# A cross-attention block: the residual add goes from VectorE to GpSimd, the layer norms' statistics follow a step later, and the expert choice takes fewer instructions

## The reference

```python
x = x + tanh(g_xattn[0]) * xattn(layernorm(x), ctx, ctx, bias, ...)     # 16 heads of 16, bias [128, 16, 128, 128]
#   scores = q_h @ k_h.T / 4 + bias;  p = softmax(scores);  out = p @ v_h   (q, k, v with low-rank terms)
x = x + tanh(g_ffn[0]) * ffn(layernorm(x))
#   expert = argmax(softmax(x @ Wg + bg));  out = gelu(x @ W1[e] + b1[e]) @ W2[e] + b2[e]
```

## Time and profile before

| | us |
|---|---|
| median of 3 runs (lowest, highest) | 1483.44 (1481.97, 1483.55) |
| the profiled execution's own time | 1482.58 |
| its span, from the first to the last instruction | 1480.4 |
| TensorE busy | 1367.4 (92%) |
| VectorE busy | 1079.3 (73%) |
| GpSimd busy | 962.8 (65%) |
| ScalarE busy | 904.5 (61%) |
| first scores start at | 33.92 |
| last scores start at | 1117.61 |

### The profile page before, as it was taken

The page is one execution under the profiler, slowest core; times in us unless marked ns, Lnnn a source line. Parts: engine busy times, 40 slices in busy tenths (PEclk is TensorE's granted clock), DMA queues, the critical chain, the costliest instruction groups (busy, mean ns, idle before and its releaser), DMA issues.

```text
span 1480.4 us, 43554 instructions
## 1 busy us (share of the span) xinstructions
PE 1367.4 (92%) x13462; PEld 1144.0 (77%) x13462; DVE 1079.3 (73%) x2591; ACT 904.5 (61%) x1915; POOL 962.8 (65%) x1062
## 2 busy tenths in 40 slices
PE   6999999999999999999999999999995589999997
PEld 4778787888788877878787778887774468888886
DVE  4888888888888888888888888888886423333333
ACT  2677777777777777777777777777764223333332
POOL 3657777777777777777777777777776234444444
PEclk7999999999999999999999999999998799999999
DMA  7455566556556556655655655655650578888884
GB/s 198 120 167 165 163 176 176 159 170 181 157 168 176 166 161 175 174 160 173 176 158 168 183 158 166 176 167 161 179 148 32 177 242 268 258 261 261 259 254 120
DMA packets 350771, 264.79 MB, mean 179 GB/s; under 512 B 18007, under 2 KB 313335, under 8 KB 350714
## 3 DMA queue, kind: packets, MB, share of 16 engines
q1 hardware_dynamic: 337130, 228.61, 54.4%
q0 software_dynamic: 13056, 34.63, 6.3%
q10 hardware_dynamic: 528, 0.84, 0.2%
HBM read 226.88 MB, written 39.22 MB: 180 GB/s over the span
## 4 chain that ended last, share of the span: by engine, by line
PE 48%; DVE 23%; issue 17%; ACT 3%; POOL 3%; SPq 3%; DVEq 1%; DMA 1%; POOLq 0%; ACTq 0%
DVE sc L829 9%; PE bank L486 8%; PE bank L637 7%; PE bank L623 7%; PE bank L479 6%; PE bank L464 5%; PE bank L566 4%; PE bank L531 2%; PE bank L516 2%; DVE st L850 2%; PE bank L612 2%; DVE x L928 2%; POOL x2n L402 2%; DVE negmax L835 2%; DVE CNT L879 2%
## 5 line engine op out<-in xcount | busy, mean ns | idle before, releaser
L381 POOL TENSOR_TENSOR sc<-sc,negmax 128x1024 f32<-128x1024 f32 x256 | 485.3, 1896 | 178.8 <-DVE negmax L835 175.8
L829 DVE TENSOR_TENSOR sc<-bank,sc 128x512 f32<-128x512 f32 x512 | 328.6, 684 | 99.9 <-PE bank L464 95.2
L835 DVE TENSOR_REDUCE negmax<-sc 128x8 f32<-128x1024 f32 x256 | 312.4, 1220 | 17.0
L685 ACT ACTIVATE PT<-bank 128x512 f32<-128x512 f32 x512 | 278.2, 598 | 0.2
L479 PE MATMUL bank<-cst,sc 128*128 128x128 f32 x2048 | 272.5, 276 | 0.0
L433 POOL DMA_INDIRECT out<-og,ids x144 | 141.7, 984 | 181.2 <-issue 158.9
L479 PEld LDWEIGHTS bank<-cst,sc 128*128 128x128 f32 x2048 | 225.5, 141 | 25.5 <-issue 25.5
L994 DVE SCALAR_TENSOR_TENSOR og<-bank,tg,sc 128x512 f32<-128x512 f32 x72 | 54.1, 751 | 196.6 <-PE bank L637 192.8
L416 POOL DMA_INDIRECT rows_dram<-x2n,slot_i x128 | 138.6, 1083 | 59.0 <-issue 55.1
L669 ACT ACTIVATE KT<-bank,bk_half,cst 128x256 f32<-128x256 f32 x256 | 123.7, 563 | 52.6 <-PE bank L486 52.6
L464 PE MATMUL bank<-KT,QT 32*128 32x256 f32 x2048 | 146.6, 400 | 1.0 <-ACT x2T L721 0.4
(11 more groups left out here) (134 smaller groups left out, 2193.3 us busy)
## 6 DMA issues: line engine op xcount, KB each, us to landing
sc<-in_bias SPq DMA_DIRECT2D x256, 512.0 KB, 4.9
xg<-rows_dram SPq DMA_DIRECT2D x72, 272.0 KB, 3.4
w_sb<-in_w SPq DMA_DIRECT2D x72, 257.0 KB, 3.9
sc<-in_w SPq DMA_DIRECT2D x72, 256.0 KB
x_sb<-in_x SPq DMA_DIRECT2D x128, 128.0 KB, 2.0
ctx_sb<-in_ctx_in SPq DMA_DIRECT2D x128, 128.0 KB, 4.9
rows_dram<-vacant SPq DMA_DIRECT2D x9, 272.0 KB, 3.1
out<-og,ids POOLq DMA_INDIRECT x144, 3.9
```

The lines of the kernel that those rows point to most:

```text
L381: nc.gpsimd.tensor_tensor(s, s, m, ALU.add).then_inc(sub_ok, 1)
L685: nc.scalar.activation(PT[:, t.slot(2), 512 * q:512 * q + 512], b_t[q % 2][:], ACT.Exp).then_inc(pt_ready, 1)
L829: nc.vector.tensor_tensor(s, b_s[q][:], s, ALU.add).then_inc(s_used, 1)
L835: nc.vector.tensor_reduce(negmax[:, t.slot(2), 8 * h:8 * h + 8], sc[:, t.slot(4), 1024 * h:1024 * h + 1024].rearrange("p (h k) -> p h k", ...
```

## The change

1. VectorE's product with the reciprocals (L922) is written to `x2` in SBUF instead of to PSUM. The residual add (L928) leaves VectorE; GpSimd does it, in place, behind its two subtractions, and signals `x2_ok` from there. TensorE's next use of that PSUM bank waits for the product (`y_ok`) alone.
2. VectorE takes the second norm's statistics not of `done` at the end of a step but of `old` in the step after, behind the bias adds of quarters 0 and 1 and ahead of the first row maximum.
3. GpSimd computes scale and shift first in its step, for lags -4 and 3 in place of -5 and 2, and subtracts the maxima after that.
4. ScalarE applies both norms behind the exponentials of quarters 0 and 1, not ahead of the OT copy.
5. The expert choice runs on the lag 4 and lag 5 steps themselves, its instructions set between VectorE's others: a maximum, a comparison, two running sums (`tensor_tensor_scan`) and a product take the place of ten instructions. The one-hot and the counts lie in two halves of `tally` that alternate.
6. In the set-up, GpSimd does three steps instead of two ahead of its memsets.

```diff
+        lmax, best = sb("lmax", [P, 4]), sb("best", [P, 4, EXPERTS])
+        run = sb("run", [P, 4 * EXPERTS])
+        tally = sb("tally", [P, 2, 44])
+        SEEN = [tally[:, 1 - g, 4:44] for g in range(2)]
+        SUMS = [tally[:, g, 0:40] for g in range(2)]
+        OH = [z.rearrange("p (e j) -> p j e", j=5)[:, 1:5, :] for z in SEEN]
+        CNT = [z.rearrange("p (e j) -> p j e", j=5) for z in SUMS]
...
         def norms_at(i, k):
 
-            which = [n for n, lag in enumerate((-5, 2)) if seq(i, k, lag)]
+            which = [n for n, lag in enumerate((-4, 3)) if seq(i, k, lag)]
             return (which[0], which[-1] + 1) if which else None
 
...
             def step(i, k):
-                cur = seq(i, k, 0)
-                if cur:
-                    subtract_max(cur, 0)
-                    subtract_max(cur, 1)
-                norms = norms_at(i, k)
+                cur, done, norms = seq(i, k, 0), seq(i, k, 2), norms_at(i, k)
                 if norms:
-                    here, row = At(i, k, U), (k - 2) % 8
-                    ahead, done = seq(i, k, -5), seq(i, k, 2)
-                    if done and done.reached(8):
-                        pool.wait_ge(x2_out[row], done.per(8, 16))
-                    if ahead:
-                        pool.wait_ge(mv_ok[0], ahead.n(1, 1))
-                    if done:
-                        pool.wait_ge(mv_ok[1], done.n(1, 1))
+                    here, row = At(i, k, U), (k - 3) % 8
+                    nxt, old = seq(i, k, -4), seq(i, k, 3)
+                    if old and old.reached(8):
+                        pool.wait_ge(x2_out[row], old.per(8, 16))
+                    if nxt:
+                        pool.wait_ge(mv_ok[0], nxt.n(1, 1))
+                    if old:
+                        pool.wait_ge(mv_ok[1], old.n(1, 1))
                     pool.nop(nofuse=True)
...
-                    pool.wait_ge(ve_ok, here.n(1, 6))
+                    pool.wait_ge(ve_ok, here.n(1, 5))
...
-                    pool.wait_ge(rs_ok, here.n(1, 6))
+                    pool.wait_ge(rs_ok, here.n(1, 5))
...
+                if cur:
+                    subtract_max(cur, 0)
+                    subtract_max(cur, 1)
+                if done:
+                    pool.wait_ge(y_ok, done.n(1, 1))
+                    nc.gpsimd.tensor_tensor(x2[:, done.slot(2), :], x2[:, done.slot(2), :], x_sb[:, done.slot(8), :],
+                                            ALU.add).then_inc(x2_ok, 1)
...
-            step(0, FIRST)
-            step(0, FIRST + 1)
+            for k in range(FIRST, FIRST + 3):
+                step(0, k)
...
-            run_steps(pool, FIRST + 2, LAST, U, LOOP, step)
+            run_steps(pool, FIRST + 3, LAST, U, LOOP, step)
...
                 ins = None
                 if old:
-                    pe.wait_ge(x2_ok, old.n(1, 1))
+                    pe.wait_ge(y_ok, old.n(1, 1))
...
-                    pe.wait_ge(cnt_ok, grp.per(4, 4, 4))
-                    mm(pos_ps, tri, OH[:], start=True, stop=False)
-                    ins = mm(pos_ps, ones, CNT[:, 0:4, :], start=False, stop=True)
+                    g = grp.k // 4 % 2
+                    pe.wait_ge(cnt_ok, grp.per(4, 1, 1))
+                    mm(pos_ps, tri, OH[g], start=True, stop=False)
+                    ins = mm(pos_ps, ones, CNT[g][:, 0:4, :], start=False, stop=True)
...
-                if old:
-                    normalise(old, 1, (k - 3) % 8, x2[:, old.slot(2), :], xn2[:, old.slot(8), :], xn2_ok, x2t_ready)
-                if nxt:
-                    normalise(nxt, 0, (k - 3) % 8, x_sb[:, nxt.slot(8), :], xn[:, nxt.slot(2), :], xn_ok, xt_ready)
                 if fin:
                     act.wait_ge(ot_ready, fin.n(1, 1))
                     if fin.reached(1):
                 if prev:
                     probs(prev, 0)
                     probs(prev, 1)
+                if old:
+                    normalise(old, 1, (k - 3) % 8, x2[:, old.slot(2), :], xn2[:, old.slot(8), :], xn2_ok, x2t_ready)
+                if nxt:
+                    normalise(nxt, 0, (k - 3) % 8, x_sb[:, nxt.slot(8), :], xn[:, nxt.slot(2), :], xn_ok, xt_ready)
                 if qry and qry.slot(2) == 0:
                     queries(qry)
                 if ky and ky.slot(2) == 0:
...
-            def pick_experts(t):
-                g = t.per(4, 1, 1)
...
-                for j in range(4):
-                    nc.vector.tensor_tensor(CNT[:, j + 1, :], CNT[:, j, :], OH[:, j, :], ALU.add).then_inc(cnt_ok, 1)
-                    dve.wait_ge(cnt_ok, t.per(4, 4, j + 1))
...
             def step(i, k):
                 cur, done, gate, ahead = seq(i, k, 0), seq(i, k, 2), seq(i, k, 4), seq(i, k, -5)
-                grp, was_grp = seq(i, k, 5), seq(i, k, 6)
+                grp, old = seq(i, k, 5), seq(i, k, 3)
                 here = At(i, k, U)
-                if grp and grp.slot(4) == 3:
-                    pick_experts(grp)
-                if was_grp and was_grp.slot(4) == 3:
-                    list_slots(was_grp)
                 if cur:
                     add_bias(cur, 0)
                     add_bias(cur, 1)
+                stats(old, 1)
+                aggregate(old, 1)
+                if cur:
                     row_max(cur, 0)
                     add_bias(cur, 2)
                     add_bias(cur, 3)
                     row_max(cur, 1)
-                if here.reached(2) and (gate or done or grp):
-                    dve.wait_ge(o_ready, here.n(1, -1))
-                    if gate and gate.slot(4) == 3:
-                        if gate.reached(4):
...
-                    if done:
-                        nc.vector.reciprocal(rden[:], o_ps[:, :, D]).then_inc(rden_ok, 1)
-                        stats(ahead, 0)
-                        dve.wait_ge(rden_ok, done.n(1, 1))
-                        y = o_ps[:, :, 0:D]
-                        nc.vector.tensor_tensor(y, y, rden[:].unsqueeze(2).broadcast_to([P, HEADS, D]),
-                                                ALU.mult).then_inc(y_ok, 1)
-                        aggregate(ahead, 0)
-                        dve.wait_ge(y_ok, done.n(1, 1))
-                        if done.reached(2):
-                            dve.wait_ge(xn2_ok, done.n(1, -1))
-                        nc.vector.tensor_tensor(x2[:, done.slot(2), :].rearrange("p (h d) -> p h d", d=D), y,
-                                                x_sb[:, done.slot(8), :].rearrange("p (h d) -> p h d", d=D),
-                                                ALU.add).then_inc(x2_ok, 1)
                 if not done:
                     stats(ahead, 0)
                     aggregate(ahead, 0)
-                stats(done, 1)
-                aggregate(done, 1)
+                if not (here.reached(2) and (gate or done or grp)):
+                    return
+                gate = gate if gate and gate.slot(4) == 3 else None
+                grp = grp if grp and grp.slot(4) == 3 else None
+                dve.wait_ge(o_ready, here.n(1, -1))
+                if gate:
+                    if gate.reached(4):
+                        dve.wait_ge(best_ok, gate.per(4))
+                    nc.vector.tensor_tensor(L[:], log_ps, bg_all[:].unsqueeze(1).broadcast_to([P, 4, EXPERTS]),
...
+                if done:
+                    nc.vector.reciprocal(rden[:], o_ps[:, :, D]).then_inc(rden_ok, 1)
+                if gate:
+                    dve.wait_ge(l_ok, gate.per(4, 1, 1))
...
+                if grp:
+                    nc.vector.tensor_tensor(where[:], where[:], OH[grp.k // 4 % 2], ALU.mult).then_inc(where_ok, 1)
+                if done:
+                    stats(ahead, 0)
+                    dve.wait_ge(rden_ok, done.n(1, 1))
+                    if done.reached(2):
+                        dve.wait_ge(xn2_ok, done.n(1, -1))
+                    nc.vector.tensor_tensor(x2[:, done.slot(2), :].rearrange("p (h d) -> p h d", d=D),
+                                            o_ps[:, :, 0:D], rden[:].unsqueeze(2).broadcast_to([P, HEADS, D]),
+                                            ALU.mult).then_inc(y_ok, 1)
+                    aggregate(ahead, 0)
+                if gate:
+                    dve.wait_ge(lmax_ok, gate.per(4, 1, 1))
+                    nc.vector.tensor_tensor(best[:], L[:], lmax[:].unsqueeze(2).broadcast_to([P, 4, EXPERTS]),
+                                            ALU.is_ge).then_inc(best_ok, 1)
+                if grp:
...
+                if gate:
+                    dve.wait_ge(best_ok, gate.per(4, 1, 1))
+                    nc.vector.tensor_tensor_scan(run[:], run_on, best[:].rearrange("p j e -> p (j e)"), 0.0,
+                                                 ALU.mult, ALU.add).then_inc(run_ok, 1)
...
+                    dve.wait_ge(run_ok, gate.per(4, 1, 1))
+                    nc.vector.scalar_tensor_tensor(out=OH[gate.k // 4 % 2],
```

(3 more changed lines are left out.)

71 lines of the change are left out of this document (30 added, 41 removed).

## The result

| | before | after |
|---|---|---|
| median, us (lowest to highest, 6 runs each) | 1483.13 (1481.37 to 1484.63) | 1491.01 (1489.27 to 1494.01) |
| ratio to before, 95% interval | | 1.0057 (1.0042 to 1.0071) |
| profiled execution: time, span | 1482.58, 1480.4 | 1489.27, 1487.4 |

A forecast was written before the change was run, and what follows sets the result against it. TensorE, 92% busy, sets the pace, with odd steps waiting on GpSimd, norms and the OT copy. Rounds of eight 68.26 against 68.77 us save 8, the end 1: 1482.6 - 9 = 1473.6, stated as 1473.5, range 1456 to 1490.

The forecast's parts named there:

- S to the first bias add: VectorE, odd step: from the start S of the step's scores to the first bias add, 1.17 us.
- what it saves is worth nothing by itself in the loop: VectorE, loop: time saved on residual add and expert choice gains nothing by itself, since TensorE sets the pace.
- five dependent instructions, at 0.22 us each: VectorE's expert choice: 2.10 us in a fourth of the steps becomes 1.1 us.
- Slower through the same line: Rival, chance 0.11: odd steps cost over 9.25 us, as when statistics enter after a drained queue; at 9.35, 1493 us.
- The OT wait goes: TensorE's 58.0 us of waits, 69 times, for ScalarE's OT copy ahead of the transposes disappear.
- The new line: Odd step: bias adds, statistics, GpSimd shifts, ScalarE norms; k copies at S + 6.02, next scores at S + 8.6.
- the prediction's own sign of being wrong: GpSimd's norms later than S + 3.4, its add above 1.1 us, or ScalarE's copies before S + 5.8.
- The waits that would show it: Odd steps: scores wait for x2T 0.8 us, P times V 0.4, 60-odd times each; ScalarE for shifts about 1 every step.
- Even steps keep 8.23 and 7.78, with 0.46 on top: TensorE: even steps keep their lengths in us; the odd step's late exponentials add a 0.46 us stall before P times V.
- GpSimd's add, 0.6 and hidden: GpSimd's 128x256 residual add takes 0.6 us, hidden with 0.5 us to spare on GpSimd and 1.0 on VectorE.
- The tail: After the last scores: expert choice 2.1 us becomes 1.1, against 0.2 to 0.3 for the add's detour; 1 us less.

The follow-up runs named there:

- the mask: Changed kernel with the slot-list mask L906 reading one input from PSUM instead of two from SBUF: 1474.64 us (0.9796), and 1475.36 us (0.9801) when run again.
- mask and reversed shifts: Changed kernel with L906 reading one input from PSUM and GpSimd's two shifts in the other order: 1469.22 us, 0.9756 of the kernel before.
- the two that should have freed the holds: Comparison reading PSUM, on L906 from PSUM plus reversed shifts (slot conversion from PSUM too): 1467.57 us (0.9760); on these plus residual on VectorE: 1453.21 us (0.9667).
- the fastest version: Changed kernel with L906 reading PSUM, residual add back on VectorE and GpSimd's two shifts reversed: 1452.52 us, 0.9663 of the kernel before.

## Why the prediction was wrong

- **The step that failed** is the first term of the line, "S to the first bias add", 1.17 us: in the odd step behind a group step it measured 2.21 (522.88 to 525.09). Behind it stands "what it saves is worth nothing by itself in the loop", by which VectorE's small instructions were taken off the path. They were priced from where they stood before, beside the norms' small operations and the scatter on GpSimd: "five dependent instructions, at 0.22 us each" for the expert choice. The mask L906, which belongs to the list of slots and not to these five, was put at nothing, without a reason. The change sets it between reciprocal and product, while GpSimd subtracts. There it takes 1.87 us, and the product, GpSimd's add and the next bias adds stand behind it. Its share is 1.4%, measured on another chip; the prediction missed by 1.2%. The price of 0.22 failed too (the comparison 1.01 us in the mean, the first scan 0.71), but no run shows that this cost time.
- **The number fell near a rival.** "Slower through the same line" had 1493 for a line that starts late, and 1491.01 came. But it gave another cause, statistics that do not enter right behind the bias adds. They did enter there (526.29, the bias adds from 525.09 for 1.27); the bias adds themselves were late. The likeness of the numbers is luck.
- **The trace of before showed it.** One comparison of the last group was caught beside a subtraction, VectorE and GpSimd of the kernel before:

```profile
1093.99 2.00 DVE L865 TENSOR_TENSOR key<-L,lmax 128x32 f32<-128x32 f32 x1
```

```profile
1092.18 3.75 POOL L381 TENSOR_TENSOR sc<-sc,negmax 128x1024 f32<-128x1024 f32 x2
```

It ends at 1095.99, the pair at 1095.93. The median of the group, 192 ns, hides it, and its mean, 249, hardly shows it; the longest, 2001, does. The Trainium skill states the rule too: by its page "SBUF — State Buffer", section "SBUF: two separate sides", a VectorE instruction in a mode with two ports, or with two SBUF inputs beside a GpSimd instruction that reads SBUF, and the GpSimd instruction take turns, and whichever starts first gets the shared ports "for the whole instruction". The runs agree where GpSimd was first, with the sizes above (1661 against 171 ns); the other order no run here shows. The prediction weighed another page and not this one.

- **The OT wait goes**: right, no wait of L540 is left.
- **The new line**: right where nothing is held. The step from 540.66 of the kernel after, GpSimd and ScalarE:

```profile
543.92 0.23 POOL L402 TENSOR_SCALAR ve<-mv 128x2 f32<-128x2 f32 x1 [0.81 <-issue]
```

```profile
546.66 1.91 ACT L679 ACTIVATE KT<-bank,bk_half,cst 128x256 f32<-128x256 f32 x4
...
548.71 0.40 ACT L731 COPY x2T<-bank 128x256 f32<-128x256 f32 x1
```

With S = 540.66, GpSimd begins at S + 3.26 (3.21 by the sum), the k copies at S + 6.00 (6.02), x2T ends at S + 8.45 (8.49), and the next scores start at S + 8.55 (8.6). In the odd step behind a group step GpSimd begins at S + 4.29 and the k copies at S + 7.11, which is the prediction's own sign of being wrong (GpSimd later than S + 3.4).
- **The waits that would show it**: of x2T up to 0.9 us, 45 times (some 0.8, 60-odd were said), of P times V 0.7 at most, 50 times (0.4), ScalarE 148.8 / 127 = 1.17 us a step (about 1). Right in place, with fewer of the first.
- **Even steps keep 8.23 and 7.78, with 0.46 on top**: measured 8.13 and 8.41 to 8.58, within 0.3 us.
- **GpSimd's add, 0.6 and hidden**: its group reads 732 ns in place of 0.6. Hidden it was not quite. Moving it back gave 1% on the change as it is (0.9835 against 0.9935), 0.5% on top of the mask (0.9755 against 0.9801) and 1% on top of mask and reversed shifts (0.9663 against 0.9756), each pair over two chips. All these chips are ones on which P times V is long in gate steps beside the add.

```profile
L416 POOL TENSOR_TENSOR x<-x,x_sb 128x256 f32<-128x256 f32 x128 | 93.7, 732 | 25.2 <-DVE x L912 25.2
```

What in the add costs this is open. It takes 0.73 us of GpSimd's queue ahead of the norms, it holds VectorE's scan and conversion (708 and 634 ns, 225 and 195 without it), and on these chips the kernels with it have the longer P times V in gate steps (1.3 to 1.6 us). No run parts the three, since the two that should have freed the holds passed them on.
- **The tail**, 1 us less forecast, 2.9 measured.
- **A slip in the sum.** 1473.6 is for the profiled execution; with the 0.9 by which the median lies above it the sum gives 1474.5, not 1473.5. It changes nothing in the above.

## What to carry to other kernels

Before a VectorE instruction is moved, look at what GpSimd does at its new place: a multiply, comparison, scan, copy or conversion of 0.17 us with all operands in SBUF can last as long as what is left of GpSimd's. Read the longest of a group beside its mean, and follow one outlier to its neighbour engine. Where such an instruction must stand there, read one operand from PSUM, and check that the hold didn't just pass to the next one.

## What the runs showed of the hardware

- **The hold.** A VectorE instruction with two SBUF inputs, or a conversion from SBUF to SBUF, that started beside a running GpSimd subtraction or add ended 0.03 to 0.07 us after that one in the rows above, up to 2.00 us where 0.19 is usual. A copy from SBUF to SBUF took 1629 ns in the mean. With an input in PSUM the multiply did not wait (171 ns, 32 of them). GpSimd is not slowed by it: the pair takes 3.75 us with and without, and the single subtractions of the kernel after 1893 to 1924 ns. Not every instruction that reads SBUF alone is held: the row maximum L845 took 1219 to 1223 ns in all 256 cases, also where the subtraction ran beside it, as at 520.33.
- **A kernel's rhythm differs between chips.** The kernel before takes 1483 us on one chip and 1503 to 1506 on four others; the changed one 1491 and 1496. So the change is 0.57% slower on the first and 0.65% faster on another. The granted clock does not explain it (0.981 and 0.978 in the profiled executions of the kernel before, 0.982 and 0.980 in those of the changed one). On a slower chip the OT wait of the kernel before no longer alternates. Two of L531's rows there, three steps apart:

```profile
505.49 0.63 PE L531 MATMUL bank<-cst,OT 128*128 128x128 f32 x4 [0.67 <-ACT OT L703]
...
532.41 0.63 PE L531 MATMUL bank<-cst,OT 128*128 128x128 f32 x4 [0.87 <-ACT OT L703]
```

In the middle of the loop it stands in seven of eight steps there (102 times over the whole, 60.8 us), where the earlier trace rows had it in odd ones alone. The changed kernel differs in its gate steps, 8.99 and 9.00 in the mean against 8.54 and 8.76 on the first chip, with the longer P times V. What tips a kernel from one rhythm to the other is open, and whether the fastest version keeps its whole 3.4% on the first chip was not measured.
